# GpSimd adds the probabilities of the five full key tiles; TensorE sums the total once

## What is computed

```python
q, k = rope(x @ w_q.T), rope(x @ w_k.T)      # 16 heads of 32 channels
v = x @ w_v.T
scores = einsum('bhqd,bhkd->bhqk', q, k) / sqrt(32)
scores = where(causal mask in blocks of 64, scores, -inf)
attn = softmax(scores, axis=-1)              # exp(...) / sum over the keys
ctx = einsum('bhqk,bhkd->bhqd', attn, v)
x = x + ctx @ w_o.T
```

## Time and profile before

| | |
|---|---|
| median of 3 runs | 710.92 us (710.17 to 711.37) |
| the profiled execution | 710.02 us |
| its span in the trace | 708.2 us |
| busy: TensorE matmul | 592.3 us (84%) |
| busy: VectorE | 443.2 us (63%) |
| busy: ScalarE | 294.4 us (42%) |
| busy: GpSimd | 157.2 us (22%) |

### The profile page before, as it was taken

The page is one execution under the profiler, slowest core; times in us unless marked ns, Lnnn a source line. Parts: engine busy times, 40 slices in busy tenths (PEclk is TensorE's granted clock), DMA queues, the critical chain, the costliest instruction groups (busy, mean ns, idle before and its releaser), DMA issues.

```text
span 708.2 us, 9858 instructions
## 1 busy us (share of the span) xinstructions
PE 592.3 (84%) x3554; PEld 219.0 (31%) x3554; DVE 443.2 (63%) x878; ACT 294.4 (42%) x597; POOL 157.2 (22%) x131
## 2 busy tenths in 40 slices
PE   0384878799999999998656687888999999999895
PEld 0232433333323222233324343333323323222252
DVE  5998459777677772014868854987776768400464
ACT  1711211146456666743306121113555557685232
POOL 1800422213123010104316124222222210000232
PEclk9987999899999999999967899998999999999899
DMA  8420332221221100000410023222212210000003
GB/s 311 184 26 0 111 112 68 82 76 46 68 69 55 37 2 1 2 1 1 178 59 1 0 66 114 89 91 67 68 46 71 66 46 2 1 1 1 1 1 118
DMA packets 35033, 41.41 MB, mean 58 GB/s; under 512 B 3026, under 2 KB 27730, under 8 KB 34986
## 3 DMA queue, kind: packets, MB, share of 16 engines
q1 hardware_dynamic: 31962, 36.23, 16.1%
q10 hardware_dynamic: 3024, 4.56, 1.8%
HBM read 23.88 MB, written 16.78 MB: 57 GB/s over the span
## 4 chain that ended last, share of the span: by engine, by line
PE 60%; DVE 28%; DMA 4%; issue 3%; ACT 2%; POOL 2%; SPq 0%; DVEq 0%; ACTq 0%
PE bank L701 11%; PE bank L673 10%; PE bank L761 9%; PE bank L752 9%; PE bank L685 7%; PE bank L644 6%; DVE rot L573 5%; DVE rmax L556 4%; PE bank L636 4%; DVE xl L500 3%; DVE stats L475 3%; DVE big L491 3%; PE bank L729 3%; DVE t L566 2%; DVE xs L510 2%
## 5 line engine op out<-in xcount | busy, mean ns | idle before, releaser
L556 DVE TENSOR_REDUCE rmax<-bank 128x1 f32<-128x512 f32 (+3 forms) x384 | 200.2, 554 | 95.9 <-PE bank L685 91.8
L403 ACT ACTIVATE big<-bank 128x512 f32<-128x512 f32 (+3 forms) x384 | 175.9, 488 | 148.9 <-PE bank L673 146.1
L685 PE MATMUL bank<-kst,qst 104*128 104x512 f16 (+3 forms) x384 | 126.0, 337 | 24.8 <-DVE rmax L556 19.4
L673 PE MATMUL bank<-qst,kst 106*128 106x512 f16 (+3 forms) x384 | 120.9, 332 | 2.3 <-ACT big L403 1.2
L333 POOL TENSOR_TENSOR t<-t,rot 128x512 f32<-128x512 f32 x32 | 40.5, 1266 | 200.3 <-DVE rot L573 200.3
L752 PE MATMUL bank<-big,ones 128*32 128x512 f32 (+3 forms) x768 | 81.8, 498 | 0.9 <-ACT cf L423 0.9
L761 PE MATMUL bank<-big,vs 128*32 128x512 f32 (+3 forms) x768 | 81.8, 498 | 0.0
L673 PEld LDWEIGHTS bank<-qst,kst 106*128 106x128 f16 x384 | 34.6, 96 | 143.0 <-ACT big L403 99.2
L343 POOL TENSOR_TENSOR cl<-cf,ch 128x512 f16<-128x512 f32 x16 | 18.5, 1157 | 203.1 <-ACT ch L429 203.1
L701 PE MATMUL bank<-xh,wh 128*128 128x512 f16 x128 | 42.0, 426 | 18.6 <-DVE xl L519 14.2
L636 PE MATMUL bank<-wt,xh 128*128 128x512 f16 x128 | 37.4, 420 | 23.6 <-DVE xl L500 23.6
(11 more groups left out here) (70 smaller groups left out, 618.8 us busy)
## 6 DMA issues: line engine op xcount, KB each, us to landing
spread<-rhl SPq DMA_DIRECT2D x32, 256.0 KB, 2.2
qst<-spread SPq DMA_DIRECT2D x16, 384.0 KB, 3.8
kst<-spread SPq DMA_DIRECT2D x16, 384.0 KB, 3.8
vs<-in_L_attn_x_dram SPq DMA_DIRECT2D x4, 1024.0 KB, 6.6
spread<-rhl SPq DMA_DIRECT2D x32, 128.0 KB, 2.1
out_dram<-xs ACTq DMA_DIRECT2D x16, 256.0 KB, 2.0
xs<-in_L_ffn_weight_dram SPq DMA_DIRECT2D x1, 1024.0 KB, 8.4
kst<-in_L_attn_w_q_dram SPq DMA_DIRECT2D x1, 1024.0 KB, 14.1
```

Of the source, the lines that this page charges most:

```text
L403: nc.scalar.activation(probs[:, st % P_PLACES, h, 0:n], pb[u % 2][:, 0:n], ACT.Exp, scale=EXP_SCALE).then_inc(s_eb, 1)
L556: nc.vector.tensor_reduce(rmax[:, at:at + 1], pa[u % 3][:, 0:n], AX.X, ALU.max, negate=True).then_inc(s_max, 1)
L673: nc.tensor.matmul(pb[u % 2][:, 0:n], kst[0:ROWS_B, g % SETS, h, j * P:(j + 1) * P], qst[0:ROWS_B, g % SETS, h, q0:q0 + n], start=True, st ...
L685: nc.tensor.matmul(pa[u % 3][:, 0:n], qst[0:ROWS_A, g % SETS, h, i * P:(i + 1) * P], kst[0:ROWS_A, g % SETS, h, half * HALF:half * HALF + ...
```

## The change

Of the second query half, GpSimd adds the probabilities of key tiles 0 to 4 (all 512 queries wide) element by element, one add per head for tiles 1 to 4: the first add of a head takes the probabilities of tiles 0 and 1, each later one the running total and the next tile. So there are 16 adds per group and 128 in both images. TensorE multiplies the four totals with the ones once (start of the PSUM accumulation), and sums tiles 5, 6 and 7 as before. The first query half is summed as before.

The totals (4 heads x 512 f32 in each partition) lie in the row tiles 4 to 7 of `xs`. Their content is written to a DRAM tensor `resid` behind the second normalize, and read back behind the last group's total; the updates of these row tiles wait for that.

The places in the k-list: GpSimd's adds ADD_LAG = 5 k-steps behind each exp, the total TOTAL_LAG = 10 behind the first head of tile 4, which is local step 42; the sums' lag goes from 5 to 7, that of P x V from 7 to 9, and with it everything that hangs on a query half's end; the output products start 2 k-steps later. An exp that writes into a place of `probs` waits, beside P x V, for the adds that read it. The release semaphores count anew.

```diff
-SUM_LAG, PV_LAG = 5, 7
+SUM_LAG, PV_LAG = 7, 9
+ADD_LAG, TOTAL_LAG = 5, 10
+LAST_ADD = 4
+ADDS = GH * LAST_ADD
-LAST_STEP = STEPS * (GROUPS + 2) + B_START + PV_LAG + 2
+LAST_STEP = STEPS * (GROUPS + 2) + B_START + max(PV_LAG + 2, TOTAL_LAG + 4) + 1
-O_START = STEPS * (GROUPS + 1) + B_START + 28
+O_START = STEPS * (GROUPS + 1) + B_START + 30
+BACK_STEP = STEPS * (GROUPS + 1) + B_START + GH * (4 + LAST_ADD) + TOTAL_LAG + 1
...
+        total = xs[:, 4:8, :]
+        resid = nc.dram_tensor("resid", (P, 4, C), F32, kind="Internal").ap()
...
# SyncE
+                sp.wait_ge(s_y, b * 24 + 16)
+                sp.dma_start(resid, xs[:, 4:8, :]).then_inc(s_spill, 16)
                 for k in range(LAST_STEP):
+                    if k == BACK_STEP:
+                        sp.wait_ge(s_spill, 16 * b + 16)
+                        sp.wait_ge(s_total, (b + 1) * GROUPS)
+                        sp.dma_start(xs[:, 4:8, :], resid).then_inc(s_back, 16)
...
# GpSimd, between L337 and L343 of a k-step
+                    if (t := b_unit(k - ADD_LAG)) and t[3] and 1 <= t[4] <= LAST_ADD:
+                        g, st, h, half, j, q0, n = t
+                        done = (b * GROUPS + g) * ADDS + GH * (j - 1) + h
+                        pool.wait_ge(s_eb, b * 192 + STEPS * g + GH * st + h + 1)
+                        if j == 1:
+                            pool.wait_ge(s_spill, 16 * b + 16)
+                            if g:
+                                pool.wait_ge(s_total, b * GROUPS + g)
+                            first = probs[:, (st - 1) % P_PLACES, h, 0:n]
+                        else:
+                            pool.wait_ge(s_add, done - GH + 1)
+                            first = total[:, h, HALF - n:HALF]
+                        pool.tensor_tensor(total[:, h, HALF - n:HALF], first, probs[:, st % P_PLACES, h, 0:n], ALU.add
+                                           ).then_inc(s_add, 1)
...
# ScalarE, ahead of an exp
+                        if st >= 4 + P_PLACES or g and st < 4:
+                            j_old, g_old = (st - 4 - P_PLACES, g) if st >= 4 else (st + 4, g - 1)
+                            if j_old <= LAST_ADD:
+                                act.wait_ge(s_add, (b * GROUPS + g_old) * ADDS + GH * max(j_old, 1))
...
# VectorE, ahead of an update of xs
+                    if r >= 4:
+                        dve.wait_ge(s_back, 16 * b + 16)
...
# TensorE
+                    if (t := pv_step(k, TOTAL_LAG)) and t[2] and t[3] == LAST_ADD:
+                        g, st, half, j, q0, n = t
+                        pe.wait_ge(s_add, (b * GROUPS + g + 1) * ADDS)
+                        pe.wait_ge(s_ln, b * 8 + 2 * g + 1)
+                        for h in range(GH):
+                            last = nc.tensor.matmul(psum[h * D:(h + 1) * D, :], ones[:, 0:D], total[:, h, :], start=True,
+                                                    stop=False, skip_group_check=True)
+                        last.then_inc(s_total, 1)
-                    if t := pv_step(k, SUM_LAG):
+                    if (t := pv_step(k, SUM_LAG)) and (t[2] == 0 or t[3] > LAST_ADD):
```

More of the change, by code:

```diff
@@ L178, in macaron @@
         s_sum = sem("s_sum")
+        s_add = sem("s_add")
+        s_total = sem("s_total")
+        s_spill = sem("s_spill")
+        s_back = sem("s_back")
         s_pv = sem("s_pv")
@@ L419, in _ @@
                         n = 2 * c[0] + c[1]
-                        act.wait_ge(s_sum, b * 48 + 12 * c[0] + 4 + 8 * c[1])
+                        act.wait_ge(s_sum, b * 8 + n + 1)
                         if n:
@@ L743, in _ @@
                         transposed += 1
-                    if t := pv_step(k, SUM_LAG):
+                    if (t := pv_step(k, TOTAL_LAG)) and t[2] and t[3] == LAST_ADD:
[7 more added lines that the diff above has]
+                    if (t := pv_step(k, SUM_LAG)) and (t[2] == 0 or t[3] > LAST_ADD):
+                        g, st, half, j, q0, n = t
+                        pe.wait_ge(s_eb, b * 192 + STEPS * g + GH * (st + 1))
+                        if j == 0 and g:
+                            pe.wait_ge(s_ln, b * 8 + 2 * g)
+                        for h in range(GH):
+                            last = nc.tensor.matmul(psum[h * D:(h + 1) * D, q0 - half * HALF:HALF], ones[:, 0:D],
+                                                    probs[:, st % P_PLACES, h, 0:n], start=(j == 0), stop=(j == 4 * half + 3),
+                                                    skip_group_check=True)
+                        if j == 4 * half + 3:
+                            last.then_inc(s_sum, 1)
+                    if t := pv_step(k, PV_LAG):
                         g, st, half, j, q0, n = t
@@ L748, in _ @@
                             pe.wait_ge(s_vs, b * TILES + TILES)
[L749 to L757, removed]
                         if j == 0 and (g or half):
```

## The result

The changed kernel takes 773.16 us (median of 4 runs, 771.63 to 774.94) against 710.54 us for the kernel before on the same chip: ratio 1.088, 95% interval 1.0855 to 1.0909. It is slower by 62.6 us; the forecast was 775 us.

A forecast was written before the change was run, and what follows sets the result against it. TensorE was taken to set the pace in the attention phases, with GpSimd nearly free. The last add of each group being late: 710.9 + 50 (waits) + 14 (TensorE's clock) = 775 us, range 745 to 806.

The forecast's parts named there:

- The price of an add: GpSimd's 128x512 f32 add, back to back: 1.23 us each, 16 per group 19.7 us.
- The release: End of each group's last GpSimd add, for which TensorE's total waits: E + 29.9, 28.6, 22.1, 22.1 in groups 0 to 3.
- E: Clock start in each group: the end of exp 20, the exp of key tile 1's first head.
- The sum of the waits: Time added by late totals: 7.5, 8.2, 5.6, 3.2 us in the second image's groups; 50 us over both images.
- the rival of the smaller loss: Work after a release runs quicker and the clock does not fall; at most 20 us come back: 741 us, 13%.
- Where TensorE stands: TensorE stands still 6 to 12 us per group ahead of the total, waiting for GpSimd's adds.
- product 42: TensorE's score product (L673) at local k-step 42 of a group; the total stands right behind it.
- The clock: TensorE's granted clock falls after each wait: 8 x 1.7 = 14 us, bounds 0 and 28.
- The edits at nothing: Spill, restore, ScalarE's new waits on adds, L337 behind adds, and later sums and P x V: costed at nothing.
- The rival that the adds are hidden: GpSimd's adds stay ahead of TensorE, so the removed sum steps' 31.7 us are gained: 679 us, 5%.
- The rival of drawn-out adds: VectorE slows GpSimd's adds to 1.44 or 1.72 us each: 802 or 838 us, 8%.

The follow-up runs named there:

- the run with eight adds: Changed kernel, only tiles 0 to 2 added on GpSimd, total last: 726.86 us; with tile 1's adds earlier and tile 2's later in GpSimd's order: 708.79 us.
- the filled waits: Changed kernel with 14 matmuls of weights ahead of TensorE's wait for the adds in each group: 760.51 us, ratio 1.070.
- narrow adds: Changed kernel, each add 64 columns wide instead of 512: 706.84 us; with tile 1's adds one k-step behind their exps, the others seven: 703.73 us.
- the kernel without adds: Kernel before, sums of key tiles 1 to 4 of the second half left out, nothing put in their place: 688.31 us, ratio 0.970.
- split places: Changed kernel with 64-column adds, tile 1's one k-step behind their exps, the others seven, total at step 42: 703.73 us, ratio 0.9895.
- 12 adds: Changed kernel, tiles 0 to 3 on GpSimd, tile 1's adds one k-step behind, others seven, total last: 710.36 us; with old lags, total at 50: 708.03 us.

## Why the prediction was right

- **The price of an add.** Eight adds in 9.83 us are one every (9.83 - 1.27) / 7 = 1.22 us; 1.23 was taken.
- **The release.** Forecast E + 29.9, 28.6, 22.1, 22.1; measured E + 30.4, 29.2, 22.6, 22.9. The first wait for L350 ended at E + 7.3, not 6.6, and L374 started at E + 4.3 in group 2 and 4.5 in group 3, not 3.7; that is all of the difference. That GpSimd is held there was tested: with the adds one k-step behind their exps the time fell by 24 us.
- **The sum of the waits.** The first exps of the second image's groups start at 518.43, 579.99, 636.23 and 679.59, before at 486.23, 537.77, 584.78 and 621.21. So groups 0, 1 and 2 take 10.0, 9.2 and 6.9 us more, and group 3, to the end of its last exp, 3.0 (42.25 against 39.26). In the first image it is 7.8, 11.5, 7.6 and 2.8. As forecast, but for the first image's group 1.
- **How near the total is.** These eight stretches hold 58.8 of the 62.6 us. With the 16 us of the clock taken off, an estimated 43 are left for what was costed at 50, and some 4 us lie outside them, where nothing was forecast. The parts were off by -7, +2 and +4 us, so that 775 came within 2 us of 773.2 is in part luck. That less than 50 was left fits what the rival of the smaller loss said, that some of the wait is caught up behind a release; but it had the clock term at nothing, and that was wrong.
- **Where TensorE stands.** This step failed in its place, not in its sum: directly ahead of the total it stood 3.0 to 4.9 us in this image (3.0 to 5.6 in the first), not 6 to 12. The forecast had TensorE at the total's place at E + 18.4, 16.5, 12.4 and 15.8 (5.3 us ahead of the old product 42); it came there at E + 27.0, 26.2, 17.8 and 19.6, because the waits that were costed at nothing came first. Over the whole of group 0 it was idle 10.9 us. In group 0 a row just ahead shows the stacked keys, which wait for L354:

```profile
562.58 0.58 PE L722 MATMUL bank<-kst,qst 104*128 104x512 f16 x1 [3.65 <-DMA kst<-spread]
```

As was said, these lie ahead of the release and add nothing while the adds are last. With a lag of one k-step they were last in groups 0 and 1, and the run with eight adds showed that they can cost much on their own: 18 us.
- **The clock.** Taken at 14 us; the granted clock behind the eight totals gives 16 us, and the filled waits gave 12.6 us back. In the changed kernel, behind the release of groups 1 and 3 (columns as above):

```profile
629.00:634.00 5.00, 4.50 (x26) 0.92 (x30) 0.75 (x2) 0.92 (x3) 0.45 (x1) 0.66 0.01 3
...
715.00:718.50 3.50, 3.50 (x15) 0.65 (x19) 0.00 (x0) 0.38 (x1) 0.00 (x0) 0.52 0.25 37
```

- **The edits at nothing.** Lags and transfers, each alone: 0.998 and 1.000. The spill landed in 3.9 us, the restore in 4.8.
- **The rival that the adds are hidden** was mis-sized: 32 sum steps are worth 22 us, not 31.7. The chain of waits gives the 0.99 us that such a step occupied. Without the steps TensorE waits 7.7 us for ScalarE's exps instead of 1.2 and 23.0 us for VectorE's maxima instead of 19.4. Nor are sums and products most of the chain, as the prediction has it: in group 0 of the second image they are 14.4% each, behind the projection L701 (20.0%) and the scores L673 (15.2%). The forecast did not rest on it, since the removed sums lay in waited time.
- **The rival of drawn-out adds** did not come: the adds took 1.25 to 1.29 us. The collision went the other way, at VectorE's cost, and took in an instruction that the prediction had left out (last section).

Open: why narrow adds at 703.7 to 706.8 us stay 15 to 18 us above the kernel without adds. VectorE's small instructions are not the reason: VectorE is busy 441.6 and 442.7 us in these two runs and 442.1 in the kernel without adds. A part is seen: with 64 columns and split places the last output products start 7.8 us after the last exp, in the kernel before and in the one without sums 6.3 us, once per image; and in groups 0 the clock was low in stretches in which it was high in the kernel without adds. The first makes 3 us at most (the run with the lags alone shows the same 7.8 us and is at 708.0); the rest was not told apart.

Open too, with a suspect: why 12 adds do no better than 8. VectorE is busy 459.6 and 461.9 us with 12 adds, 448.8 with 8 and 443.2 in the kernel before, and TensorE's waits for its maxima come to 24.0 and 28.8, 24.3 and 19.4 us. No run tests that by itself. No version was found that clearly beats the kernel before.

## What to carry to other kernels

Work that is moved to an idle engine costs its length at the place where its end is waited for: add up the receiving engine's whole queue from the input's arrival to the consumer's place, including what that engine waits for on behalf of others, and compare it with the time the consumer needs to get there. Then order that queue: adds placed ahead of an instruction that waits anyway, and behind one that others wait for, took 18 us off with the same instructions. Look at what else stands behind the moved work, too: once the adds came earlier here, the stacked keys held TensorE. The gain is to be measured with the work left out, before the mover is built: here 22 us, not the 31.7 us of the chain.

## What was not expected of the hardware

VectorE's instructions of 4 to 8 columns beside GpSimd's adds. In the kernel before, L587 and L588 (now L624 and L625) took 0.17 us each, never more than 0.173. In the changed kernel, second image, group 0 (VectorE):

```profile
558.47 1.20 DVE L624 TENSOR_SCALAR mparts<-rmax 128x8 f16<-128x8 f32 x1
559.70 1.18 DVE L625 SCALAR_TENSOR_TENSOR mparts<-rmax,mparts 128x8 f16<-128x8 f32 x1
```

The first has one SBUF input only, and is held for about the length of an add as the second is. GpSimd's run of eight adds (555.91 to 565.74, above) went on beside them: each got in after one add. Over the whole kernel VectorE is busy 13.2 us longer than before (456.4 against 443.2). "SBUF — State Buffer" in the Trainium skill, section "Who interferes with whom", counts `tensor_scalar` among the operations that can take the shared ports in a 2-port mode; the trace agrees with it, and the prediction had left it out.

In the run with a lag of 1 one VectorE instruction, the small one with two SBUF inputs (L622, 0.16 us as a rule), waited for several adds in a row. VectorE and GpSimd there:

```profile
283.28 5.82 DVE L622 TENSOR_TENSOR rmax<-rmax 128x4 f32<-128x4 f32 x1
```

```profile
276.81 12.27 POOL L368 TENSOR_TENSOR xs<-xs,big 128x512 f32<-128x512 f32 x10
```

It started in the middle of the run of ten adds and ended at 289.10, with the last one (289.08). That is the exception: every other small instruction that was held in this run took 1.22 us at most, and what makes the difference is not shown. It has a price: TensorE stood 4.26 us ahead of the transpose of these maxima and came to the total 3.2 us behind the last add:

```profile
289.61 0.26 PE L777 MATMUL bank<-ident,mparts 128*16 128x128 f16 x1 [4.26 <-issue]
```

The other surprise is that filling a wait with matmuls whose result nobody reads made the kernel 12.6 us faster.
